# Splitting K into two f16 halves: ACT and DVE straight from PSUM, in place of a f32 copy by ACT and two products by POOL

## The reference, cut to what matters

```
q = layernorm(x) @ qw.T + qb          # 16 batches, 56 tokens, 128 wide, 16 heads of 8
k = ctx @ kw.T + kb                   # 16 batches, 1500 keys
v = ctx @ vw.T + vb
scores = where(mask == 0, -1e9, (q * DH**-0.5) . k)     # per head, 56 x 1500
out = softmax(scores) @ v ; x += tanh(g0) * (out @ ow.T + ob)
x += tanh(g1) * moe(layernorm(x))     # 8 routed experts, 2 chosen, one shared
```

## Time and profile before

| | |
|---|---|
| median of the runs | 580.48 us (579.09 to 580.92, 3 runs) |
| the profiled execution | 578.95 us, its span 577.1 us |
| busy, TensorE matmuls | 509.8 us (88% of the span) |
| busy, DVE | 399.5 us (69%) |
| busy, ACT | 330.3 us (57%) |
| busy, POOL | 140.5 us (24%) |
| mean granted TensorE clock | 0.956 of full speed |

### The profile page before, as it was taken

One profiled execution on the slowest core, in us unless ns is written; L12 is line 12 of the kernel. 1 busy time (PEld: TensorE's weight loads), 2 busy tenths in 40 slices (PEclk: granted clock), 3 DMA queues, 4 the chain that ended last, 5 costly groups with the idle time before them and its releaser, 6 DMA issues.

```text
span 577.1 us, 15690 instructions
## 1 busy us (share of the span) xinstructions
PE 509.8 (88%) x6779; PEld 353.5 (61%) x6779; DVE 399.5 (69%) x753; ACT 330.3 (57%) x411; POOL 140.5 (24%) x128
## 2 busy tenths in 40 slices
PE   1365999999999999999999999999899469999993
PEld 1123667676766767676676767667677355777772
DVE  6357567687766768776776878677674556778756
ACT  2211566656566665656666565665657228788781
POOL 4051514325061432506153250605000000000000
PEclk9869899999999999999999999999999768999997
DMA  4999869886686867668586766847000500210001
GB/s 151 197 246 243 176 167 178 218 184 134 151 190 150 172 152 185 131 153 185 150 173 156 175 136 156 183 84 163 3 3 2 147 0 2 71 42 2 1 2 32
DMA packets 39805, 72.82 MB, mean 126 GB/s; under 512 B 4638, under 2 KB 26271, under 8 KB 39736
## 3 DMA queue, kind: packets, MB, share of 16 engines
q1 hardware_dynamic: 38456, 70.90, 54.1%
q10 hardware_dynamic: 1280, 0.92, 0.7%
HBM read 24.28 MB, written 0.46 MB: 43 GB/s over the span
## 4 chain that ended last, share of the span: by engine, by line
PE 75%; DVE 12%; DMA 5%; issue 4%; ACT 2%; SPq 1%; POOL 1%; ACTq 0%; POOLq 0%; DVEq 0%
PE ring L336 14%; PE pv L374 12%; PE st L357 11%; PE ring L281 9%; PE ring L319 8%; PE st L661 7%; DVE max_part L501 7%; PE ring L700 5%; DMA ctxT<-in_ctx 3%; PE pv L380 3%; DVE recip L530 2%; DMA ident_h<-in_c_ident_h 2%; PE pv L700 1%; SPq L265 1%; PE ring L909 1%
## 5 line engine op out<-in xcount | busy, mean ns | idle before, releaser
L501 DVE TENSOR_REDUCE max_part<-ring 112x1 f32<-112x512 f32 (+1 forms) x384 | 245.3, 673 | 104.2 <-PE ring L336 102.5
L454 ACT ACTIVATE probs<-st 128x896 f32<-128x896 f32 x192 | 175.6, 915 | 104.1 <-PE st L357 101.3
L336 PE MATMUL ring<-keys,qrs 121*112 121x512 f16 (+1 forms) x384 | 141.2, 392 | 8.4 <-DVE max_part L501 4.0
L357 PEld LDWEIGHTS st<-qrs,keys 121*128 121x128 f16 (+1 forms) x1536 | 89.7, 102 | 42.9 <-issue 13.9
L357 PE MATMUL st<-qrs,keys 121*128 121x112 f16 (+1 forms) x1536 | 108.8, 214 | 2.0 <-ACT qrs L443 2.0
L561 POOL TENSOR_TENSOR k_hi<-k_raw,zero 128x512 f16<-128x512 f32 (+1 forms) x45 | 45.9, 1019 | 219.6 <-ACT k_raw L422 219.0
L374 PE MATMUL pv<-probs,v_ext 128*32 128x168 f32 (+1 forms) x1536 | 94.5, 318 | 0.3 <-DVE sums L521 0.2
L281 PE MATMUL ring<-ctxT,w_qkv 128*128 128x512 f32 (+1 forms) x94 | 56.5, 688 | 13.3 <-DMA ctxT<-in_ctx 13.1
L336 PEld LDWEIGHTS ring<-keys,qrs 121*112 121x112 f16 x384 | 46.6, 131 | 32.2 <-DVE max_part L501 26.2
L374 PEld LDWEIGHTS pv<-probs,v_ext 128*32 128x32 f32 (+1 forms) x1536 | 30.3, 108 | 46.3 <-issue 33.8
L422 ACT ACTIVATE k_raw<-ring,biases 128x512 f32<-128x512 f32 (+1 forms) x45 | 30.5, 677 | 46.3 <-PE ring L281 44.7
(11 more groups left out here) (113 smaller groups left out, 374.4 us busy)
## 6 DMA issues: line engine op xcount, KB each, us to landing
ctxT<-in_ctx SPq DMA_DIRECT2D x16, 750.0 KB, 4.2
keys<-mask_add SPq DMA_DIRECT2D x32, 375.0 KB
keys<-k_hi SPq DMA_DIRECT2D x32, 375.0 KB, 6.1
keys<-k_lo SPq DMA_DIRECT2D x32, 375.0 KB, 7.0
keys<-mask_add SPq DMA_DIRECT2D x32, 281.2 KB
mask_raw<-in_mask SPq DMA_DIRECT2D x15, 375.0 KB, 3.7
up_w<-in_up_w SPq DMA_DIRECT2D x9, 256.0 KB, 2.8
down_w<-in_down_w SPq DMA_DIRECT2D x9, 256.0 KB, 3.2
```

The source lines that it names most:

```text
L336: nc.tensor.matmul(ring[0:QW, m % 2, 0:width(c)], qrs[0:ROWS, w, p, :, :].rearrange("r h q -> r (h q)"), keys[0:ROWS, w, p, chunk(c)], sta ...
L357: mm = nc.tensor.matmul(st[0:m, j % 2, p // 4, QW * (p % 4):QW * (p % 4 + 1)], keys[0:ROWS, u, p, j * P:j * P + m], qrs[0:ROWS, u, p, :, : ...
L454: nc.scalar.activation(probs[0:m, j % 3, :].rearrange("p (h c) -> p h c", h=2), st[0:m, j % 2, :, 0:HQ // 2], ACT.Exp).then_inc(s["exps_do ...
L501: nc.vector.tensor_reduce(max_part[:, p, c:c + 1], ring[0:QW, m % 2, 0:width(c)], AX.X, ALU.max).then_inc(s["max_read"], 1)
```

## The change

In every unit ACT writes `k_hi` (f16) from PSUM where it wrote `k_raw`, and DVE computes (misc + bias) - k_hi to `k_lo` from the same bank. POOL's two products go, and so does the semaphore `k_raw_stored`. Its waits move: TensorE now waits for `k_lo_made` before it writes `misc` again (chunks 1 and 2, and the small matmul of `pe_any`). The wait for the keys placed earlier (the DMAs that read k_hi and k_lo) moves from POOL to ACT and DVE, at chunk 0. In `dve_unit` the product stands after the first maximum of steps 0, 1 and 2 and before the second.

```diff
             elif not known(k, -1):
-                pe.wait_ge(s["k_raw_stored"], NCH * (k + 1) + c)
+                pe.wait_ge(s["k_lo_made"], NCH * (k + 2) + c)
...
             if not known(k, -1):
-                pe.wait_ge(s["k_raw_stored"], NCH * (k + 2))
+                pe.wait_ge(s["k_lo_made"], NCH * (k + 3))
             pe.wait_ge(s["any_row_done"], k + 3)
...
             act.wait_ge(s["k_made"], NCH * (k + 2) + c + 1)
-            if not known(k, -1):
-                act.wait_ge(s["k_lo_made"], NCH * (k + 1) + c + 1)
-            nc.scalar.activation(k_raw[:, chunk(c)], misc[:, 0:width(c)], ACT.Identity,
-                                 bias=k_bias).then_inc(s["k_raw_stored"], 1)
+            if c == 0:
+                act.wait_ge(keys_placed[buf(b, 1)], 64 * (lap(b, 1) + 1))
+            nc.scalar.activation(k_hi[:, chunk(c)], misc[:, 0:width(c)], ACT.Identity,
+                                 bias=k_bias).then_inc(s["k_hi_made"], 1)
...
+        def dve_k_lo(dve, b, c):
+            k, u, t = b
+            dve.wait_ge(s["k_hi_made"], NCH * (k + 2) + c + 1)
+            if c == 0:
+                dve.wait_ge(keys_placed[buf(b, 1)], 64 * (lap(b, 1) + 1))
+            nc.vector.scalar_tensor_tensor(out=k_lo[:, chunk(c)], in0=misc[:, 0:width(c)], scalar=k_bias,
+                                           in1=k_hi[:, chunk(c)], op0=ALU.add,
+                                           op1=ALU.subtract).then_inc(s["k_lo_made"], 1)
...
                 for m in scores[0:1]:
                     dve_max(dve, b, m)
+                if j in K_STEPS and has(k, 2):
+                    dve_k_lo(dve, b, K_STEPS.index(j))
...
-        def pool_keys(pool, b, c):
...
             if has(k, 2):
-                for c in range(NCH):
-                    pool_keys(pool, b, c)
```

More of the change, by code:

```diff
@@ L174, in flamingo_kernel @@
         mask_abs_done any_row_done any_spread any_done mask_ready qrs_made
-        k_made k_raw_stored k_hi_made k_lo_made v_made v_stored
+        k_made k_hi_made k_lo_made v_made v_stored
         scored max_read max_merged max_turned max_copied
```

## The result

The changed kernel takes 613.51 us (median of 4 runs, 611.92 to 614.71) against 580.48: a ratio of 1.057, 95% interval 1.054 to 1.061. It is 33.0 us slower; the forecast was 611.5. The profiled execution's span is 610.9 us.

What follows compares the result with a forecast made beforehand. TensorE's chain was taken to bound each 25.30 us unit; 28.1 (13 x 2.16) + 2.7 (unit 0) + 1.0 (unit -1) = 31.8 on 578.95 gave 610.8, stated as 611.5 us; range 600 to 620.

Steps and rivals of the forecast that it cites:

- The removed work: ACT's step stays 687 ns, POOL loses two products per chunk, the waits for placed keys cost nothing: 0 us.
- The product, 0.75 and 0.71 us, 0.67 of DVE's time: DVE's added product for 512 and 476 columns; three a unit take 2.0 us, against 6.8 us idle.
- the upper bound: Steady unit up to about 2.9 us longer if reading two memories beside running matmuls slows a product to 0.95.
- DVE's busy time: Expected sign in the changed trace: DVE up by 45 x 0.74 = 33 us busy.
- POOL's loss of 95: Expected sign in the changed trace: POOL's busy time down by about 95 us, from 90 products.
- The moved wait: TensorE waits for DVE's product behind a maximum: 0.76 + 0.78 at two re-used banks, 0.62 at score 7; 2.16 us a unit.
- A: Rival: only the two bank waits cost, the maxima catch up; 1.54 us a unit, 601.5 us; chance 0.10.
- B: Rival: DVE's idle time, 6.8 us a unit, swallows the added product; 579 to 582 us; chance 0.05.
- C: Rival: in start-up unit -1, losing POOL's products between ACT and the context load saves 1.9 us; 577 us; chance 0.04.
- D: Rival: stalls drop TensorE's clock to half level in steps 0 to 3 of each unit; some 736 us; chance 0.03.
- The start: Units -1 and 0, before the steady units: +1.0 us for unit -1 and about 2.7 us for unit 0.
- the wrong path out of unit -1: Claimed k_lo's end in unit -1 releases SP's key DMAs, then the context load that lets unit 0 start; +1.0 us.

Runs made afterwards that it cites:

- the narrow product: The changed kernel with DVE's product covering only 64 of the 512 (476) columns of each chunk, all waits kept; 593.83 us, ratio 1.023.
- the old start: The changed kernel with the way of before (f32 copy by ACT, two products by POOL) in units -1 and 0; 608.03 us, ratio 1.049.
- the stall filled: The changed kernel with 12 small matmuls ahead of TensorE's wait for k_lo at chunks 1 and 2, unit -1 only; 611.47 us, ratio 1.055.

## Why the prediction was right, point by point

**The removed work, at 0.** Right. ACT's step is 687 ns in both, and the profile shows no wait of ACT, DVE or TensorE for the key DMAs. ACT's spare time was tested by giving it 45 more instructions.

**The product, 0.75 and 0.71 us, 0.67 of DVE's time.** Right: means of 741 and 704 ns, and 257.47 - 256.81 = 0.66 to the next instruction. The rows of the first batch were the same operation and carried it; the slower product that the upper bound allowed for, 0.95, did not show. Only DVE's busy time was overstated as a sign, 33 us for a measured 27.6, in part because rows that overlap at their ends are counted once (45 x 0.08 = 3.6 of the 5.7 us; the rest is open); POOL's loss of 95 was measured as 96.7.

**The moved wait.** Right to 0.02 us at each of its three places, as laid over the chain above. The period came out at 27.46 with 2.16 forecast and 2.16 measured. The experiments confirm its two halves: 0.88 us for DVE's load with no bank wait (0.93 by the same walk), and 1.28 on top for the release behind the maximum, of which 1.04 come back when the product goes first.

**Rivals.** The product is indeed shorter on DVE than on POOL, but 0.71 against 1.09 us is a factor of 1.5 and not of two, and it bought nothing. A (1.54 a unit) falls with the period. B (idle time swallows it) falls with the product twice: 7 us idle a unit, and 1.94 more all the same. C's place was real, POOL's chain in unit -1, but its sign was wrong there, too: the new way lengthens that unit. D, the clock, is wrong in the steady units (1.00 throughout) and so is its 736 us.

**The start, mis-sized.** The sum had 1.0 for unit -1 and 2.7 for unit 0; measured are 60.69 - 57.42 = 3.3 and (89.58 - 60.69) - (82.75 - 57.42) = 3.6, together 6.8 and not 3.7. The step that failed is "By the same walk the first product ends at 37.2 (...), the second at about 41.1 and the third at about 44.0". The first two came as said (37.22 and 41.16). The third ended at 44.94: the walk took chunk 2's key matmul at full clock, as before, and it ran at the half level (1.95 us), as did V's first matmuls behind it (1.71 us on the chain). D's mechanism was real, in units -1 and 0. The granted clock of the same stretch in the kernel with the narrow product, in the one with the product first and in the one without TensorE's wait says what goes with it:
```profile
38.00:46.00 8.00, 7.03 (x11) 2.24 (x11) 4.13 (x9) 1.34 (x2) 0.00 (x0) 0.50 0.94 201
```
```profile
38.00:46.00 8.00, 5.87 (x11) 1.69 (x9) 4.79 (x9) 1.34 (x2) 0.00 (x0) 0.50 0.99 198
```
```profile
38.00:46.00 8.00, 5.79 (x18) 2.19 (x17) 8.00 (x15) 1.34 (x2) 1.89 (x1) 0.93 0.94 195
```
It stays at 0.50 in the kernels in which TensorE stands idle for DVE there, even with the narrow product, and rises in the ones in which it doesn't (1.00 in the kernel before, 0.91 with the old start). With the stall filled, unit -1 takes 25.70 us against 24.53 before (57.42 - 32.89), 1.2 more where 1.0 was forecast.

The prediction also had the wrong path out of unit -1. It let the third context load end last; in the changed trace unit -1's own chain of scores and maxima does, up to 59.22, and the key matmul at 60.69 does not wait for the context. That is not the clock's doing alone, since it is the same in the kernel with the filled stall.

The error is small in the total (3.1 of 33), and partly hidden by the 1.1 us that the last stage was shorter. That part is luck: from unit 14's start (unit 13's and one period) to the end the profiles of all these kernels lie between 163.8 and 166.4 us, and what moves it is open.

## What to carry to other kernels

When an operation moves onto an engine that has idle time, don't compare its length with the idle time: walk one period and see what it stands behind, and who waits for the buffer that it reads. With a single buffer, the release can be worth more than the operation: here a second reader put behind an unrelated instruction cost 1.3 us a unit beyond its load, and putting it first in the queue gave 1.0 back. An f32 copy that frees the bank early, with the rest left to an engine that nobody waits for, was the better trade here. Whether a bank for each chunk, as in the first batch, would leave only the 0.88 us of load was not tried.

## What the runs showed of the hardware that was not expected

In these kernels a stall mattered more while TensorE was at the half level than later. In steady units three stalls of 0.6 to 0.7 us left the granted clock at 1.00. In unit -1, behind a wait of 10.27 us for the first context load, it was 0.50 from 38 to 46 us with stalls of 1.54 and 1.01 us (and with 0.93 and 0.71 when the product goes first), where the kernel before had 1.00; with the stalls filled it was 0.68.

DVE's product of f32 from PSUM with f16 and the one of f32 from SBUF with f16 both take 0.74 us for 512 columns, and with 64 columns it takes 0.275: 0.47 us for 448 columns, and some 0.2 (0.275 less 64 columns at that rate) that don't depend on them.
